# Square blocks in the spectral mixing, the bias in the last feature's place, and low halves made by TensorE and ScalarE in a two-layer transformer kernel

## The reference, cut to what matters

```python
x = x + spectral_conv(ln_c(x), kernel_base)        # 32 x 32 kept Fourier modes
t = to_tokens(x)                                   # 32768 tokens of 64 features
t = t + ffn(ln_t(t), router_w0, router_b0, expert_w0, expert_b0)
x = from_tokens(t)
x = x + depthwise_conv(ln_c(x), kernels)           # 64 channels, taps up to 29 x 29
t = to_tokens(x)
t = t + ffn(ln_t(t), router_w1, router_b1, expert_w1, expert_b1)

# spectral_conv: at mode (i, j): Y = kernel_base[f_i**2 + f_j**2] @ X   (64 x 64; away from row and column 16
#   the imaginary part cancels in the real result)
# ln_t: (t - mean) / sqrt(var + eps), without gain or shift, so its 64 features sum to zero
# ffn: p = softmax(t @ router_w + router_b); the two best of 8 experts, shares scaled to sum 1;
#      y_e = t @ expert_w[e] + expert_b[e]; the sum over the two of share * y_e
```

## Time and profile before

| | |
|---|---|
| median of 3 runs (lowest to highest) | 941.23 us (940.68 to 942.5) |
| the profiled execution, and its span | 941.57 us, 939.8 us |
| PE, DVE, ACT, POOL busy, share of the span | 86%, 82%, 58%, 60% |
| mixing (PE L1498) | 82.6 to 117.2 us |
| experts of layer 0, experts of layer 1 | about 187 to 440 us, about 693 to 939 us |
| convolution (PE L1704) | about 449 to 677 us |

### The profile page before, as it was taken

The page is one execution under the profiler, slowest core; times in us unless marked ns, Lnnn a source line. Parts: engine busy times, 40 slices in busy tenths (PEclk is TensorE's granted clock), DMA queues, the critical chain, the costliest instruction groups (busy, mean ns, idle before and its releaser), DMA issues.

```text
span 939.8 us, 23972 instructions
## 1 busy us (share of the span) xinstructions
PE 807.8 (86%) x9242; PEld 654.8 (70%) x9242; DVE 774.9 (82%) x1421; ACT 545.1 (58%) x1111; POOL 567.3 (60%) x504
## 2 busy tenths in 40 slices
PE   5996888667999898875899999999848889999987
PEld 5995877634666665543899999999725566666654
DVE  5757688879999999999887677675687999998884
ACT  2467485778787877321444444444268777878621
POOL 2780201247799998896654244340116889999998
PEclk9998576979999999999899999999957999999999
DMA  9988200021887777783787877878100101101111
GB/s 371 369 260 284 70 1 2 2 53 79 321 333 313 317 301 295 291 321 121 260 282 249 283 271 251 284 267 275 42 1 1 46 24 46 46 23 46 47 45 45
DMA packets 48291, 163.06 MB, mean 174 GB/s; under 512 B 9425, under 2 KB 9937, under 8 KB 46033
## 3 DMA queue, kind: packets, MB, share of 16 engines
q1 hardware_dynamic: 48208, 161.96, 47.6%
HBM read 93.46 MB, written 68.49 MB: 172 GB/s over the span
## 4 chain that ended last, share of the span: by engine, by line
PE 32%; POOL 32%; DVE 19%; issue 10%; DMA 3%; ACT 3%; SPq 1%; POOLq 0%; DVEq 0%; ACTq 0%
PE pair L1704 24%; POOL R L573 18%; POOL R L583 11%; DVE R L906 5%; DMA X<-x_rows 3%; PE pair L1498 3%; DVE R L662 3%; DVE R L835 2%; DVE work L662 2%; PE pair L1719 1%; DVE R L846 1%; ACT pair L1251 1%; DVE R L829 1%; PE pair L1629 1%; DVE X L1071 1%
## 5 line engine op out<-in xcount | busy, mean ns | idle before, releaser
L906 DVE TENSOR_TENSOR R<-pair,R 128x896 f32<-128x896 f32 x256 | 275.5, 1082 | 26.7 <-PE pair L1612 26.1
L573 POOL TENSOR_TENSOR R<-R 128x768 f32<-128x768 f32 x128 | 231.9, 1812 | 70.8 <-DVE R L906 70.8
L1704 PE MATMUL pair<-R 128*128 (+4 forms) x2880 | 227.2, 243 | 9.5 <-DVE R L984 9.2
L1704 PEld LDWEIGHTS pair<-R 128*128 128x128 f16 x2880 | 224.2, 98 | 12.8 <-issue 10.3
L1611 PE MATMUL pair<-work,R 128*128 128x448 f16 x512 | 186.5, 364 | 45.1 <-DVE R L906 44.2
L1251 ACT ACTIVATE pair<-X,work 128x64 f32<-128x64 f32 x480 | 166.4, 393 | 57.6 <-DVE R L846 55.2
L1612 PE MATMUL pair<-work,R 128*128 128x448 f16 x512 | 185.5, 362 | 0.0
L583 POOL TENSOR_TENSOR R<-R 128x512 f32<-128x512 f32 x128 | 164.6, 1286 | 10.0
L1373 ACT COPY R<-R 128x1152 f32<-128x1152 f32 x64 | 81.9, 1283 | 117.3 <-PE pair L1704 117.3
L999 DVE COPY R<-R 128x1152 f32<-128x1152 f32 x64 | 94.6, 1479 | 63.7 <-PE pair L1704 63.0
L1629 PE MATMUL pair<-R,ident_sb 128*128 128x256 f32 x496 | 131.3, 388 | 0.6 <-ACT pair L1297 0.4
(11 more groups left out here) (138 smaller groups left out, 1243.2 us busy)
## 6 DMA issues: line engine op xcount, KB each, us to landing
taps_halves<-R SPq DMA_DIRECT2D x128, 458.5 KB, 3.6
R<-taps_halves SPq DMA_DIRECT2D x64, 917.0 KB, 4.7
X<-x_tok SPq DMA_DIRECT2D x4, 2048.0 KB, 17.8
out<-X SPq DMA_DIRECT2D x15, 512.0 KB, 2.7
R<-spec_pairs SPq DMA_DIRECT2D x16, 272.0 KB, 5.2
X<-x_rows SPq DMA_DIRECT2D x4, 1024.0 KB, 11.3
R<-x_chan SPq DMA_DIRECT2D x4, 1024.0 KB, 14.3
X<-x_rows SPq DMA_DIRECT2D x2, 2048.0 KB, 27.4
```

What stands on the lines that cost most here:

```text
L573: pool.tensor_tensor(pr[:, :, 192:384], pr[:, :, 0:192], pr[:, :, 192:384], ALU.add).then_inc(half_ready, 1)
L906: dve.tensor_tensor(pr.rearrange("p t (e c) -> p t e c", c=C), pair[p % 2][:, :].rearrange("p (t e c) -> p t e c", t=2, c=C)[:, :, 0:NE - ...
L1704: mm = pe.matmul(acc[:, y0:y1, x0:x1, :], blocks[i % 2][:, ks, 2 - y, 1 - x, :], src[:, y0 + y:y1 + y, x0 + x:x1 + x, :], start=(ks == 0 a ...
```

## The change

**Mixing.** A matrix is loaded and split once, on partitions 0 to 63; a DMA from SBUF to SBUF carries both halves over to partitions 64 to 127, shifted by 64 columns, and PE waits for it (`k_shifted`). There are four slots in place of three. The modes (a, b) and (b, a) go through one matmul of 32 columns in place of two of 16. The matrices stand in an order of 4 x 4 blocks of frequencies, a PSUM bank each, so that each step finishes a bank. `x_tok` is loaded behind all steps. Turning uses banks 2 to 5 and starts when all but the last two banks are split. POOL clears the slots in four pieces in place of two.

**Bias.** The last of the 64 normalised features is minus the sum of the others, so it is dropped: its row of weights is subtracted from the other 63 on DVE, and its place holds 1 in the high half and 0 in the low half, with the bias as the row. Both matmuls use `u`; `vh`, its copy on ACT and its memsets on POOL are gone. One of DVE's 7 steps on the weights is gone.

**Low halves.** From octet 11 of a layer on (21 of 32), PE adds minus the high half onto the normalised values in PSUM (`lower_part`, with a negative identity), and ACT copies what is left (`take_low`). The first 11 octets stay with DVE.

```diff
...
+            for t in range(4):
+                load_pairs(t)
             for t in range(NSTEP):
-                if t < 3:
-                    sp.wait_ge(c_dft, 20 + 2 * t)
-                else:
-                    sp.wait_ge(k_low, 2 * (t - 2))
...
+                sp.wait_ge(k_low, t + 1)
+                row = k_flat[t % 4]
+                sp.dma_start(row[64:128, 64:4352], row[0:64, 0:4288]).then_inc(k_shifted[t % 4], 16)
+                if t + 4 < NSTEP:
+                    load_pairs(t + 4)
...
-                if n == 18:
-                    pool.wait_ge(c_dft, 16)
-                    pool.memset(R1[:, 2304:6656], 0.0).then_inc(zeros_ready, 1)
...
+                if n in (20, 24, 28, 31):
+                    i = (20, 24, 28, 31).index(n)
+                    pool.wait_ge(c_dft, 18 + 4 * i)
+                    pool.memset(k_flat[i].bitcast(F32), 0.0).then_inc(zeros_ready, 1)
...
             for t in range(NSTEP):
-                pe.wait_ge(k_low, 2 * t + 2)
-                row = k_row[t % 3]
+                pe.wait_ge(k_shifted[t % 4], k_in_count(t))
+                row = k_row[t % 4]
                 for i, (a, b) in enumerate(matrices(t)):
-                    if a != b:
-                        mix(mixed_at(b, a), lambda s: row[:, s, i, :], freq(b, a))
-                    mm = mix(mixed_at(a, b), lambda s: row[:, s, i, :], freq(a, b))
-                    if b == 15 and a % 2 == 1:
+                    mm = mix(both_mixed(a, b), lambda s: row[:, s, i, :], both_freqs(a, b))
+                    if (a, b) == SYMMETRIC[BANK_ENDS[t] - 1]:
                         mm.then_inc(mixed, 1)
...
-            pe.wait_ge(mixed_low, NMIX)
+            pe.wait_ge(mixed_low, NMIX - 2)
...
+            def take_low(layer, k, j):
+
+                act.wait_ge(lowered, layer * (4 * NCHUNK - LOWERED_FROM) + 4 * k + j - LOWERED_FROM + 1)
+                act.copy(halves_of(j)[:, :, 1, 0:BIAS], tile_columns(xn_psum)).then_inc(tok_low, 1)
...
-                act.copy(u[q][:, at].bitcast(F32), src)
-                act.copy(vh[q][0:64, at].bitcast(F32), src[0:64]).then_inc(parts_copied, 1)
+                act.copy(u[q][:, at].bitcast(F32), src).then_inc(parts_copied, 1)
...
+            def lower_part(layer, k, j):
+
+                n = (layer * NCHUNK + k) * 4 + j
+                pe.wait_ge(tok_high, n + 1)
+                pe.matmul(tile_columns(xn_psum), minus_ident16, halves_of(j)[:, :, 0, 0:BIAS], start=False, stop=True,
+                          skip_group_check=True).then_inc(lowered, 1)
...
                         sum_quad(layer, k if g >= 0 else k - 1, q if g >= 0 else 1 - q, g % NQUAD)
+                    if following and p in LOW_AT[LOW_AHEAD:]:
+                        lower_part(layer, k + 1, LOW_AT.index(p))
+                    if normed and p in LOW_AT[:LOW_AHEAD]:
+                        lower_part(layer, k + 2, LOW_AT.index(p))
                     expert_pair(layer, k, q, p)
...
```

More of the change, by code:

```diff
@@ L35, with frequency_pairs @@
 TAP_SCALE = 256.0
+def frequency_pairs():
+    blocks = ((0, 1), (0, 2), (0, 3), (1, 2), (1, 3), (0, 0), (1, 1), (2, 3), (2, 2), (3, 3))
+    return [(4 * i + a, 4 * j + b) for i, j in blocks for a in range(4) for b in range(a if i == j else 0, 4)]
 def spectral_constants():
@@ L183, in metaformer @@
         zeros_ready = sem("zeros_ready")
-        k_in = [sem(f"k_in{i}") for i in range(3)]
+        k_in = [sem(f"k_in{i}") for i in range(4)]
+        k_shifted = [sem(f"k_shifted{i}") for i in range(4)]
         last_in = sem("last_in")
@@ L313, in matrices, with bank_place @@
             return SYMMETRIC[PER_STEP * t:PER_STEP * t + PER_STEP]
-        def finished_banks(t):
-            return [i for i in range(8) if (2 * i + 1, 15) in matrices(t)]
+        def bank_place(a, f):
+            i, j = a // 4, f // 4
+            if i == j:
+                at = BANK_BLOCKS.index((i - i % 2, i - i % 2)), i % 2
+            else:
+                at = BANK_BLOCKS.index((min(i, j), max(i, j))), int(i > j)
+            return at[0], 256 * at[1] + 64 * (a % 4) + 2 * (f % 4)
         def k_in_count(t):
-            return 32 * (t // 3 + 1)
+            return 16 * (t // 4 + 1)
         def c_dft_bank(n):
@@ L630, in _ @@
                 if layer:
-                    pool.wait_ge(blocks_ready, C)
-                    pool.wait_ge(low_blocks_ready, C)
-                for q in range(2):
-                    if layer and q:
-                        pool.wait_ge(convolved, C)
-                    pool.memset(vh[q][64:128, :].bitcast(F32), ONES).then_inc(ones_ready, 1)
-                    pool.wait_ge(ones_ready, 2 * layer + q + 1)
-                if layer:
+                    pool.wait_ge(convolved, C)
+                    bias_columns()
                     pool.wait_ge(conv_copied, C)
@@ L812, in mixed_low_part @@
                 dve.wait_ge(mixed_high, mixed_count(item))
-                dve.scalar_tensor_tensor(out=low_, in0=src, scalar=DOWN1, in1=high_, op0=ALU.mult, op1=ALU.subtract
-                                         ).then_inc(mixed_low, 1)
+                views = [(low_, src, high_)]
+                if not isinstance(item, str):
+                    views = [tuple(m[:, h] for m in views[0]) for h in range(2)]
+                for low_, src, high_ in views:
+                    last = dve.scalar_tensor_tensor(out=low_, in0=src, scalar=DOWN1, in1=high_, op0=ALU.mult,
+                                                    op1=ALU.subtract)
+                last.then_inc(mixed_low, 1)
             for t in range(NSTEP):
-                for i in finished_banks(t):
-                    mixed_low_part(i)
-                if t + 3 < NSTEP:
-                    row_low(t + 3)
+                mixed_low_part(t)
+                if t + 4 < NSTEP:
+                    row_low(t + 4)
                 if t == LAST_AFTER:
@@ L1567, in _ @@
             pe.wait_ge(turned_read_v, 8)
+            for i in range(4):
+                pe.matmul(xn_psum[:, i * P:(i + 1) * P], ident16_sb, ident16_sb, start=(i == 0), stop=(i == 3),
+                          skip_group_check=True)
             for g in range(32):
@@ L1582, in turn_tokens @@
                 n = (layer * NCHUNK + k) * 4 + j
+                if k == 0 and j == 0:
+                    pe.wait_ge(ones_ready, layer + 1)
                 pe.wait_ge(tok_low, n + 1)
@@ L1730, in _ @@
                         turn_tokens(layer, 0, 0, j)
-                pe.wait_ge(ones_ready, 2 * (layer + 1))
                 pe.wait_ge(ident_ready, 1)
```

227 lines of the change are left out of this document (127 added, 100 removed).

## The result

The changed kernel takes **961.2 us** (median of 4 runs, 958.72 to 965.37); the kernel before takes 941.87 beside it. It is slower by the ratio 1.0209 (95% interval 1.0162 to 1.0256). The forecast was 947, its range 920 to 959: the sign was right, the size was missed by 14 us, and the time lies 2 us outside of the range. The profiled execution took 965.37 us, the longest of the four and 4.2 above the median, with a span of 963.0 against 939.8 before; the 23.2 us between the spans are divided up here. Starts are those of DVE's first multiplication in a chunk (L938, before L906).

The account below looks back on a forecast made before the run. DVE was taken to bound full expert chunks, POOL 2.3 us behind. Mixing -14.1, turning -2.5, clearing -0.8, circle +27, chunk 0 -1.9, chunk 6 -1.7, weights -0.4 gave +5.6 on 941.57: 947 us, range 920 to 959.

Parts of the forecast that it names:

- The circle: Full expert chunks: PE and ACT wait on each other, 7.96 or 7.47 us a turn; ten chunks 27 us more (24 to 30).
- the 0.4 for exp_second: Expert chunks: exp_second on ACT waits for a DVE gate step after pair 10, adding about 0.4 us, 31.3 a chunk.
- The mixing's work: PE's matmuls in the mixing: 408 at 28.5 ns plus 246 at 27.4, 18.4 us (17.9 to 20.8).
- Rival (3): Mixing: a matmul of 32 columns takes two of 16, 54.8 ns, 10.7 us more, 958; 6%.
- The mixing's waiting: Mixing: PE waits 2 us, before step 4, for a shift of about 3.8 us; mixing 20.5 us, 14.1 less.
- 6.8 us of waiting for matrices: Mixing of the kernel before: 34.6 us, read as 27.8 of matmul work and 6.8 waiting for split matrices.
- The tokens are moved: price nothing: Token loads moved to about 95 us: land before 125, first reader at about 136, so no cost.
- Chunk 0: Chunk 0 and ahead of it: ACT's second copy before the transposes goes, 1.9 us less (0 to 4).
- Chunk 6: Experts' chunk 6: one DVE low half goes, POOL enters layer 1's without backlog; 1.7 us less (0 to 3).
- rival (4): Mixing: shifts queue behind each other, PE waits at every step; gain 6 us in place of 14, 955; 6%.
- Rival (1): Experts: the circle does not close; chunks fall to POOL's bound, 26.8 us, ten 17.5 less, 902; 15%.
- Rival (5): Experts: waits cost PE its full clock; PE's part of a turn doubles, 15.8 us a chunk, past 1090; 2%.

## Why the prediction was right in its sign and wrong in its size

**The circle: right.** By its own segments: `copy_sum` to the end of the high half 3.22 us (818.19 to 821.41; forecast 3.22), a turn 7.89 (7.96), a steady chunk 30.88 (31.3 with the 0.4 for exp_second, 30.9 without; that 0.4 did not come). The four runs that take it out, open it or tighten it move the chunk each time. The ten chunks still came out at +31.1, above the bound of 30, through a slip in the sum: a steady chunk of after (31.3) was multiplied by ten and set against a total of before that holds three heavier chunks (29.6 to 30.0 where the others take 28.1). After, those three take 33.3 to 33.6. Chunk against chunk it is 10 x 2.8 and 3 us for the heavier ones.

**The mixing's work: right within its bounds.** 32 columns took 31.4 ns at half clock (51 in 1.60 us, PEclk 0.50), where 28.5 was taken with bounds of 27.4 and 34.4. PE's five groups add up to 20.4 us, where the forecast had 18.4 (17.9 to 20.8). The row for the 51:

```profile
88.40:90.00 1.60, 1.60 (x51) 1.60 (x51) 0.93 (x1) 0.11 (x1) 0.00 (x0) 0.50 1.04 262
```

It is no matter of the clock: in the kernel that splits twice the first 204 matmuls, all of 32 columns, start 31 ns apart from 87.36 to 93.68, although the granted clock rose to 1.00 on the way (1.00 from 91.4 to 93.8). Rival (3), 54.8 ns, falls. The Trainium skill's rule on lines of few elements (page "SBUF — State Buffer", section "Door 1: The DMA port swizzle") brought no such doubling here; the row decides.

**The mixing's waiting: wrong, and this is the step that failed.** The prediction put "2 us of waiting", with a shift of 3.8 us (3.6 to 4.7). Measured: 5.8 us for shifts, 3.1 of a gap, and 2.5 of another ahead of the turning, which was to start sooner. So the mixing took 29.3 us and not 20.5 (34.6 before), and from its end to the experts it was 1.2 us longer, not 2.5 shorter. Three errors made it.

- *The shift was priced by its latency alone, not by its rate.* It lands after 8.3 us, not 3.8: the first two, with little beside them, took 4.4 us each, the six behind them 7.1 to 10.9. Eight of 536 KB, with four loads and the experts' weights between them, keep the DMA engines about full from 73 to 100 us (6.04 MB in all, 201 GB/s over 70 to 100), longer than PE works on the mixing. The price was taken from transfers of like size between SBUF and `taps_halves`. The rate of a transfer from 64 partitions to 64 was never asked for. The same section of the Trainium skill says it in its first part: partitions 0 to 63 reach only 8 of the 16 ports, some 218 GB/s, half of the full rate. The trace agrees: 191 to 204 GB/s in windows with shifts alone (92 to 96 and 96 to 100 us). By the page's rate a shift is 2.5 us of transfer and eight are 20, an estimate; by the 191 to 204 GB/s measured, 2.7 to 2.9 us and 22 to 23. Such a sum would have shown the queue.
- *"6.8 us of waiting for matrices" in the kernel before was no such waiting.* The time line has groups of 143, 256, 128 and 487 matmuls with gaps between them that no semaphore ends; the two groups in the middle are these:

```profile
89.99 7.02 PE L1498 MATMUL pair<-R 128*128 128x16 f16 x256 [3.59 <-issue]
98.55 3.58 PE L1498 MATMUL pair<-R 128*128 128x16 f16 x128 [1.54 <-issue]
```

  I read the earlier trace rows beside the splits of the earlier trace rows and made a cause of the neighbourhood; the brackets name no engine. So splitting sooner could not save them.
- *"The tokens are moved: price nothing"* asked only when the tokens are needed, not what they run beside. They moved from the time ahead of the mixing (57.6 to 86.1 us) to its end and the turning (96.7 to 122.9), where the gaps of 3.10 and 2.51 us stand.

What the gaps are. Each stands 143 matmuls in, or a multiple of 128 behind that (with as many weight loads), in every kernel whose rows stand here; only the one ahead of the turning of the changed kernel comes one matmul sooner. 8 MB beside the mixing made 0.49 us into 8.4. The traces also have packets of 16384 bytes on an instruction queue (q8; that it is PE's follows from the times), and they bear it out: over this kernel, the one before and the eleven of the experiments, all 34 gaps above 0.3 us in the mixing and right behind it that end with "issue" end 1.3 to 1.6 us after such a packet has ended. And the next packet waits for the data: it starts 1.0 to 1.3 us after PE has gone on where nothing else is transferred, and 3.6 to 4.3 us after where 400 to 430 GB/s run. So these gaps are waits for instructions that stand behind data in the DMA engines. With nothing else under way the instructions are there some 3.6 us after PE has begun a block (1.1 us, 1.1 for the packet and 1.4 behind it, an estimate from these times), about as long as 128 matmuls of 28 ns take, so any delay shows. How the DMA engines share out their time is not shown. The Trainium skill has this instruction memory (page "Runtime: NRT & Kernel Launch", section "Instruction fetch mechanics"): it is refilled in blocks of 16 KiB, 256 instructions, which fits 128 matmuls with 128 weight loads. The same section calls the cost at the end of a block mostly hidden; here it was up to 4.1 us, and the measurement decides.

**The smaller terms.** Chunk 0 gave 2.9 us for 1.9. Chunk 6 gave nothing for 1.7: in layer 1 it takes 27.42 us against 26.81 before, and 26.70 with `lower_part` a pair later, so the circle holds there too; in layer 0 it stays at 29.7, and why is open. The mixing's start came 0.8 us earlier, the convolution's stretch 0.8 shorter.

**The rivals.** What came is rival (4), "shifts queue, the mixing gains 6": its place is right, and PE waited for shifts at three steps of eight. Its size (6.1 us at the mixing's end) is right in part by luck: of the 8.9 us that PE waited inside the mixing, 3.1 are a gap that the rival does not have. It had 6% and deserved more, since the shift had no row. Its 955 comes to about the median with the 4 that the chunks took above the forecast and the 2.4 of chunk 6; the profiled execution is 4.2 longer. Rival (1) is what the circle's removal gives: 26.9 a chunk against its 26.8. Rival (5) did not come (clock 1.00 in the window of a chunk), but with the longer waits of `lower_part` a pair sooner the clock did fall, to 0.87.

One number needs a word: five kernels share the changed mixing and all that lies before the experts, and their experts start between 188.9 and 194.4 us. So this part varies by 5.5 us between executions, about as much as the changed kernel's own runs do. The difference stands in the mixing, which ends between 109.6 and 114.8; from there it is 79.3 to 80.5 us in all five. What sets the size of its waits in an execution is open.

## What to carry to other kernels

When an operation moves from one engine to another between two in-order loops, write down the circle it closes, edge by edge, with durations from the trace; such a sum came within 2% in the forecast, and one place later in a table was worth 41 us. Price a new transfer by its rate and its partitions, and add up all of them on the queue, before its latency is hidden behind anything. A gap on PE that the profile ends with "issue", at a fixed count of matmuls, was a wait for its instructions here: look at the packets of the instruction queue, keep large transfers away from stretches of many small matmuls, and don't credit such gaps to whatever waits beside them.

## What the runs showed of the hardware

- A transfer within SBUF from 64 partitions to the other 64, in rows of 8576 bytes, ran at 191 to 204 GB/s; the tokens over 128 partitions at 401 to 437.
- Matmuls of 32 columns in runs of two elements started 31 ns apart, at a granted clock of 0.50 and of 1.00 alike; those of 16 took 27.4 to 28.0 at 0.50.
- Between its gaps the mixing of before and after had a granted clock of 0.50, except for the first 143 matmuls of before (0.78), though the transform ahead of it had 0.97 to 1.00.
- PE lost up to 2.85 us for each 128 matmuls while 422 GB/s ran beside it, and 0.49 us once in 654 while nearly nothing did. Such a gap ended 1.3 to 1.6 us after a packet of 16384 bytes on its instruction queue.
